# First attention pass of a four-layer graph network: where the second half of a batch is packed and turned

## The chip, the cores and the metric

The kernel runs on one core of one Trainium2 chip. The metric is the device time of one execution in microseconds; three executions of the kernel before gave 8632.77, 8639.03 and 8645.94 us, median 8639.03 us.

## The reference, cut to what matters

Four graph layers run one after another over 6250 nodes of 128 features and 106250 edges, each followed by a residual and a layer norm. The second one, a graph attention with 4 heads of 64 features, is the one the change touches:

```python
h = (x @ W).reshape(n, HEADS, HID)                      # 4 heads x 64
e = jax.nn.leaky_relu(a_src[src] + a_dst[dst], 0.2)
m = jax.ops.segment_max(e, dst, num_segments=n)
ex = jnp.exp(e - m[dst])
denom = jax.ops.segment_sum(ex, dst, num_segments=n)
msg = h[src] * (ex / denom[dst])[:, :, None]
agg = jax.ops.segment_sum(msg, dst, num_segments=n)
```

## The kernel before, in words

Edges were sorted earlier into chunks of 128 by their target's tile of 128 nodes. `attend_running` (line 1222) goes over all chunks once, in 58 batches (`NB`) of 8 pairs of chunks (`BP`), 16 chunks a batch (`BC`). It keeps a running maximum per target, so that for each batch two kinds of work are in flight: the maxima and scores of batch b, and the messages and sums of batch b-1. Five instruction streams are written out by hand, one for each engine, and are tied together by semaphores; each engine runs its stream strictly in the order written.

**GpSimd** gathers the source rows of a batch by 16 indirect DMAs (L1350), into a ring of three batches; each half of 8 waits until the sums of the batch three before have left the ring. **SyncE** loads hot bytes (L1323) and bit lines (L1331).

**For the maxima of batch b**: ScalarE copies the source part of a half batch out of the gathered rows (`pack(b, n)`, L1514, n = 0 or 1 for the half), TensorE transposes it in two matmuls (`turn(b, n)`, L1600), ScalarE copies the result to SBUF (`line(b, n)`, L1523). Then, for each pair a of 0 to 7, TensorE spreads the lines over all lanes in 8 matmuls (`spread(b, a)`, L1614; pairs 0 to 3 need `line(b, 0)`, pairs 4 to 7 `line(b, 1)`), VectorE reduces the 128x1024 result (`reduce`, L1390) and takes it into the running maximum (`top`, L1398). PSUM holds two pairs, so a spread waits for the reduce two before. After the last pair VectorE makes the shifts (`shift`, L1404 to L1412, and `change`, L1421), TensorE expands them to the edges in 48 small matmuls (`expand`, L1625), VectorE makes the scores (L1443 to L1449) and ScalarE the exponentials (L1544, L1545). ScalarE also widens the hot bytes (`widen` L1531, `hot` L1536).

**For the sums of batch b-1**: ScalarE multiplies three heads of each chunk by their weights (`message(b - 1, a)`, L1553, 6 instructions for a pair, 48 for a batch), VectorE the fourth (L1454); TensorE sums a pair in 4 float matmuls (`total(b - 1, a)`, L1640), VectorE adds the sum to the accumulator (`add`, L1462). A total waits for its messages and for the add two before.

The order in one turn of the loop before the change:

- ScalarE: messages 0 and 1, `pack(b, 1)`, message 2, `line(b, 1)`, messages 3 to 7, `pack(b + 1, 0)`, `hot(b)`, `line(b + 1, 0)`, `widen(b + 1)`, a small exponential, then the exponentials of batch b.
- TensorE: for a = 2 to 7 `spread(b, a)` and `total(b - 1, a - 2)`, with `turn(b, 1)` ahead of spread 4; then totals 6 and 7, `turn(b + 1, 0)`, spreads 0 and 1 of b + 1, `expand(b)`.
- VectorE: for a = 2 to 7 reduce a, top a-1, add a-2; top 7, the shifts, adds 6 and 7, reduces 0 and 1 of b + 1, the scores, its part of the messages, `rescale` (L1431, L1434).

Of the kernel before, what the change touches and what calls it, by code (L numbers as in the profile page):

```python
# [83 lines left out]
def gnn_resnorm_kernel(nc, x_in, src_in, dst_in, type_in, rfeat, relw, loopw,  # L84
# [3 lines left out]
    with ctx:  # L88
# [1133 lines left out]
        def attend_running(name, f, t_tab, a_src, a_dst, most):  # L1222
# [6 lines left out]
            BP = 8  # L1229
            BC = 2 * BP  # L1230
            HALF = BC // 2
            NB = NPAIR // BP
# [5 lines left out]
            with Phase() as ph:  # L1238
# [51 lines left out]
                def rows_gathered(b):  # L1290
                    return (b // ZR + 1) * 16 * HALF

                def loaded_pairs(b, slots):
                    return (b // slots + 1) * 16 * BP

                def turned(b, n):
                    at = n * P
                    return ps[0:PR, 6 + b % 2, at:at + P].bitcast(bf16)
# [17 lines left out]
                with nc.Block() as block:  # L1316
                    @block.sync
                    def _(sp):
                        def bytes_in(b):
                            if b >= HR:  # L1320
                                sp.wait_ge(s_hot, b - HR + 1)
                            for a in range(BP):
                                sp.dma_start(hb[:, b % HR, a], hb_tab[:, bass.ds(places[b][a], 2), :])\  # L1323
                                  .then_inc(s_hb[b % HR], 16)

                        def bits_in(b):
                            if b >= 2:
                                sp.wait_ge(s_spread, (b - 1) * BP)
                            for a in range(BP):
                                at = PR + a % 2 * 2 * LB  # L1330
                                sp.dma_start(lines[at:at + 2 * LB, b % 2, a // 2, :],  # L1331
                                             bit_tab[bass.ds(places[b][a], 2)].rearrange("c k e -> (c k) e"))\
                                  .then_inc(s_bits[b % 2], 16)

                        places = {}
                        for b in range(-2, NB):
                            if b + 2 < NB:
                                places[b + 2] = registers([mybir.EngineType.SP], pair_at, b + 2, NCH - 2)
                                bytes_in(b + 2)
                            if 0 <= b + 1 < NB:  # L1340
                                bits_in(b + 1)
                                places.pop(b + 1)
# [159 lines left out]
                    @block.scalar  # L1502
                    def _(act):
                        for n in range(2):
                            act.wait_ge(s_pt, n + 1)
                            nc.scalar.activation(pick[:, n * HALF:(n + 1) * HALF, :].rearrange("p m e -> p (m e)"),
                                                 ps[0:LR, 4 + n, :].bitcast(bf16), ACT.Copy).then_inc(s_pick, 1)

                        def pack(b, n):
                            at = 2 * b + n  # L1510
                            act.wait_ge(s_gath[b % ZR][n], rows_gathered(b))
                            if at >= 2:
                                act.wait_ge(s_turn, at - 1)
                            nc.scalar.activation(  # L1514
                                parts[:, n, :].rearrange("p (c w) -> p c w", w=HP),
                                ring[:, b % ZR].bitcast(bf16)[:, n * HALF:(n + 1) * HALF, 2 * W:2 * RW], ACT.Copy)\
                              .then_inc(s_pack, 1)

                        def line(b, n):
                            act.wait_ge(s_turn, 2 * b + n + 1)  # L1520
                            if b >= 2:
                                act.wait_ge(s_spread, (b - 1) * BP)
                            nc.scalar.activation(  # L1523
                                lines[0:PR, b % 2, n * QB // 2:(n + 1) * QB // 2, :].rearrange("p q e -> p (q e)"),
                                turned(b, n), ACT.Copy).then_inc(s_line, 1)

                        def widen(b):
                            act.wait_ge(s_hb[b % HR], loaded_pairs(b, HR))
                            if b >= WR:
                                act.wait_ge(s_exp, b - WR + 1)  # L1530
                            nc.scalar.activation(wide[:, b % WR], hot_bytes(b, 0), ACT.Copy).then_inc(s_wide, 1)  # L1531

                        def hot(b):
                            if b >= WR:
                                act.wait_ge(s_sum, (b - WR + 1) * BP)
                            nc.scalar.activation(hots[:, b % WR], hot_bytes(b, P), ACT.Copy).then_inc(s_hot, 1)  # L1536

                        def fading(b):
                            act.wait_ge(s_diff, b)
                            nc.scalar.activation(fade[:, b % 2, :], fade[:, b % 2, :], ACT.Exp).then_inc(s_fade, 1)  # L1540

                        def exponential(b):
                            act.wait_ge(s_sc, 3 * b + 3)
                            nc.scalar.activation(factors(b), score[:, b % 2], ACT.Exp).then_inc(s_e, 1)  # L1544
                            nc.scalar.activation(ring[:, b % ZR, :, hf:W], score[:, b % 2], ACT.Exp).then_inc(s_e, 1)  # L1545

                        def message(b, a):
                            if a == 0:
                                act.wait_ge(s_e, 2 * b + 2)
                            for c in range(2 * a, 2 * a + 2):  # L1550
                                for h in range(ACT_HEADS):
                                    r = ring[:, b % ZR, c, h * f:(h + 1) * f]
                                    last = nc.scalar.activation(r, r, ACT.Copy,  # L1553
                                                                scale=ring[:, b % ZR, c, hf + h:hf + h + 1])
                            last.then_inc(s_ma, 1)

                        pack(0, 0)
                        line(0, 0)
                        widen(0)
                        for b in range(NB + 1):  # L1560
                            for a in range(BP):
                                if b < NB and a == 2:
                                    pack(b, 1)
                                if b < NB and a == 3:
                                    line(b, 1)
                                if b >= 1:
                                    message(b - 1, a)
                            if b + 1 < NB:
                                pack(b + 1, 0)
                            if b < NB:  # L1570
                                hot(b)
                            if b + 1 < NB:
                                line(b + 1, 0)
                                widen(b + 1)
                            if 1 <= b < NB:
                                fading(b)
                            if b < NB:
                                exponential(b)
                            if b == NB - 1:
                                act.wait_ge(s_of, 1)  # L1580
                                nc.scalar.activation(own[:], own[:], ACT.Exp).then_inc(s_og, 1)

                    @block.tensor
                    def _(pe):
# [64 lines left out]
                        for b in range(NB + 1):  # L1649
                            for a in range(2, BP):  # L1650
                                if b < NB:
                                    if a == BP // 2:
                                        turn(b, 1)
                                    spread(b, a)
                                if b >= 1:
                                    total(b - 1, a - 2)
                            if b >= 1:
                                total(b - 1, BP - 2)
                                total(b - 1, BP - 1)
                            if b + 1 < NB:  # L1660
                                turn(b + 1, 0)
                                spread(b + 1, 0)
                                spread(b + 1, 1)
                            if b < NB:
                                expand(b)
                            tiles.pop(b, None)
                            if b + 1 < NB:
                                tiles[b + 1] = registers(PE_ENGINE, pair_tile, b + 1, NT)
# [973 lines left out]
```

## Time and profile before

| | before |
|---|---|
| median of three executions | 8639.03 us |
| the profiled execution, its own time | 8636.3 us |
| its span in the trace | 8634.5 us |
| first exponential of the pass to the last | 2496.02 to 3747.14 us |
| busy share over the whole span: TensorE, VectorE, ScalarE, GpSimd | 62%, 66%, 35%, 71% |

The shares are means over a dozen stages with different limits; the pass in question takes about 15% of the span. A time in the trace counts from the start of the span. A row of a stretch gives its ends and its length, then the busy time of TensorE's matmuls, its weight loads, VectorE, ScalarE and GpSimd with their instructions in brackets, the granted clock of TensorE as a share of full speed, the share of busy DMA engines and GB/s. What stands in brackets at the end of a row of the timeline is the idle time of the engine just before it, and what ended it.

### The profile page before, as it was taken

The page shows a single profiled execution, that of the slowest core. Times are in us where ns is not written, and L with a number is a line of the kernel's source. Part 1 is how long each engine was busy: PE and PEld are TensorE (multiplying, and loading weights), DVE is VectorE, ACT ScalarE, POOL GpSimd, SP SyncE. Part 2 cuts the span into 40 slices and gives each one's busy share as a digit, 9 for nine tenths or more (in the row PEclk, how much of TensorE's full clock was granted, in tenths as well). Part 3 has the DMA queues.
Part 4 walks back from the last instruction along what each step waited for, and adds up shares of the span by engine and source line. Part 5 has one row for each costly group of instructions (what it writes and reads, how often), then busy time and mean ns, then how long its engine had stood idle before and what let it go on. Part 6 is the DMA issues. An engine that isn't in the chain of part 4 may idle for free. (4 is left out here: it accounts for less than half of the span.)

```text
span 8634.5 us, 137054 instructions
## 1 busy us (share of the span) xinstructions
PE 5332.5 (62%) x37070; PEld 4681.0 (54%) x37070; DVE 5717.4 (66%) x14044; ACT 2990.4 (35%) x6453; POOL 6115.6 (71%) x5619
## 2 busy tenths in 40 slices
PE   0991014444368888854444425666569898989896
PEld 0340013333356666643333315565569898989896
DVE  9660025555577777774444455555579898989898
ACT  2000002000047777742222222222246565655564
POOL 4777767777547767726777727777768787878785
PEclk6995555555577777776666657667889999999998
DMA  1771025565644444533333334444467676767674
GB/s 42 274 308 45 2 52 130 131 145 131 109 120 132 130 128 130 122 59 89 81 80 82 82 44 129 129 129 129 126 163 221 190 222 189 221 188 219 189 222 138
DMA packets 963001, 1176.45 MB, mean 136 GB/s; under 512 B 286475, under 2 KB 845279, under 8 KB 949199
## 3 DMA queue, kind: packets, MB, share of 16 engines
q1 hardware_dynamic: 806638, 864.50, 32.7%
q0 software_dynamic: 155616, 303.19, 16.3%
q8 instruction: 324, 5.31, 0.3%
q14 instruction: 423, 3.46, 0.1%
HBM read 897.16 MB, written 269.96 MB: 135 GB/s over the span
## 5 line engine op out<-in xcount | busy, mean ns | idle before, releaser
L2560 PE MATMUL ps<-u,wide_r 128*128 x9280 | 1140.1, 277 | 129.5 <-issue 88.7
L2391 POOL TENSOR_TENSOR msg_r<-zo_r,share_r 128x1024 f32<-128x1024 f32 x580 | 1122.0, 1934 | 101.6 <-DVE share_r L2450 45.8
L2560 PEld LDWEIGHTS ps<-u,wide_r 128*128 128x128 f32 x9280 | 1091.8, 193 | 131.4 <-issue 131.4
L2572 PE MATMUL ps<-msg_r,hots_r 128*128 128x128 f32 x9280 | 1140.6, 276 | 24.5 <-POOL msg_r L2391 23.3
L1350 POOL DMA_INDIRECT ring_e<-t_tab,src_p x928 | 878.2, 946 | 386.2 <-issue 267.2
L2133 POOL DMA_INDIRECT z_r<-x_tab,src_row x880 | 856.0, 973 | 417.0 <-issue 267.9
L2572 PEld LDWEIGHTS ps<-msg_r,hots_r 128*128 128x128 f32 x9280 | 1081.8, 192 | 33.5 <-POOL msg_r L2391 32.5
L295 POOL DMA_INDIRECT rec_tab<-pay,row_i x831 | 805.6, 969 | 375.1 <-issue 274.6
L583 POOL DMA_INDIRECT ring<-y_tab,y_row x880 | 839.5, 954 | 306.4 <-issue 264.5
L1753 POOL DMA_INDIRECT ring_e<-t_tab,src_row x880 | 830.4, 944 | 271.9 <-issue 271.9
L2399 POOL TENSOR_TENSOR prod_r<-prod_r 128x512 f32<-128x512 f32 x580 | 734.4, 1266 | 320.5 <-DVE prod_r L2422 307.0
L842 PE MATMUL ps<-ring,hots 128*128 128x129 f32 x1760 | 453.2, 438 | 697.5 <-issue 533.3
L842 PEld LDWEIGHTS ps<-ring,hots 128*128 128x128 f32 x1760 | 394.3, 329 | 756.5 <-issue 618.1
L2275 PE MATMUL ps<-unit,wide_r 128*128 x1760 | 399.1, 419 | 583.2 <-ACT wide_r L2240 578.8
L2461 DVE TENSOR_TENSOR u_sum<-ps,u_sum 128x128 f32 x2320 | 671.8, 290 | 103.1 <-PE ps L2572 22.2
L2422 DVE TENSOR_TENSOR prod_r<-ps,zo_r 128x1024 f32<-128x1024 f32 x580 | 705.4, 1216 | 34.4 <-PE ps L2560 30.9
L2275 PEld LDWEIGHTS ps<-unit,wide_r 128*128 128x128 f32 x1760 | 368.9, 319 | 603.5 <-issue 603.5
L1640 PE MATMUL ps<-ring_e,hots_e 128*128 128x260 f32 x1856 | 627.3, 471 | 94.4 <-ACT ring_e L1553 89.5
L1553 ACT ACTIVATE ring_e<-ring_e 128x64 f32<-128x64 f32 x2784 | 681.4, 334 | 1.9
L2512 ACT ACTIVATE wide_r<-zo_r 128x1024 f32<-128x1024 uint8 x580 | 605.4, 1044 | 97.8 <-PE ps L2560 62.0
L1390 DVE TENSOR_REDUCE high_e<-ps 128x4 f32<-128x1024 f32 x464 | 560.7, 1219 | 100.1 <-PE ps L1614 98.8
L2524 ACT ACTIVATE hots_r<-zo_r 128x1024 f32<-128x1024 uint8 x580 | 603.5, 1040 | 0.0
(317 smaller groups left out, 9472.1 us busy)
## 6 DMA issues: line engine op xcount, KB each, us to landing
zo_r<-zo_tab SPq DMA_DIRECT2D x2320, 192.0 KB, 2.8
y_tab<-wide SPq DMA_DIRECT2D x100, 1024.0 KB, 3.9
zo_tab<-z_r SPq DMA_DIRECT2D x110, 512.0 KB
hot_bytes_e<-hb_tab SPq DMA_DIRECT2D x464, 64.0 KB
dl_b<-dl_tab SPq DMA_DIRECT2D x220, 128.0 KB, 3.7
zo_tab<-hot_bytes SPq DMA_DIRECT2D x220, 128.0 KB
hb_tab<-hot_bytes SPq DMA_DIRECT2D x220, 128.0 KB
hot_bytes_e<-hb_tab SPq DMA_DIRECT2D x55, 512.0 KB
```

What stands on the lines that cost most here:

```text
L295: nc.gpsimd.indirect_dma_start(out=rec_tab, out_offset=bass.IndirectOffsetOnAxis(ap=row_i[:, j:j + 1], axis=0), in_=pay[:, j, :], in_offse ...
L583: nc.gpsimd.indirect_dma_start(out=ring[:, s, c, 0:width], out_offset=None, in_=table, in_offset=bass.IndirectOffsetOnAxis(ap=rows[:, q * ...
L842: last = nc.tensor.matmul(sum_of(s, c), hots[:, s, c, :], ring[:, s, c, :], start=True, stop=True)
L1350: nc.gpsimd.indirect_dma_start(out=ring[:, b % ZR, c, :], out_offset=None, in_=t_tab, in_offset=bass.IndirectOffsetOnAxis(ap=src_p[:, b * ...
L1753: nc.gpsimd.indirect_dma_start(out=ring[:, b % ZR, c, :], out_offset=None, in_=t_tab, in_offset=bass.IndirectOffsetOnAxis(ap=src_row[:, b ...
L2133: nc.gpsimd.indirect_dma_start(out=z[:, g % ZR, c, :], out_offset=None, in_=x3_tab, in_offset=bass.IndirectOffsetOnAxis(ap=src_row[:, g * ...
L2275: last = nc.tensor.matmul(ps[:, 2 * (g % 2) + c // 4, c % 4 * D:(c % 4 + 1) * D], wide[:, g % WR, c, :], unit[:, bass.ds(tiles[at // CQ, a ...
L2391: nc.gpsimd.tensor_tensor(msg[:, g % WR].rearrange("p c (k d) -> p c k d", d=CD), z_of(g).rearrange("p c (k d) -> p c k d", d=CD), share[: ...
L2399: nc.gpsimd.tensor_tensor(prod[:, :, 0:CD // 2], prod[:, :, 0:CD // 2], prod[:, :, CD // 2:CD], ALU.add).then_inc(s_half, 1)
L2422: v.tensor_tensor(prod[:].rearrange("p (c k) d -> p c (k d)", k=CAPS), up, z_of(g), ALU.mult).then_inc(s_prod, 1)
L2560: last = nc.tensor.matmul(ps[:, 2 * (g % 2) + c // 4, c % 4 * D:(c % 4 + 1) * D], wide[:, g % WR, c, :], u[:, bass.ds(tiles[g % NO % 4 * O ...
L2572: last = nc.tensor.matmul(ps[:, 4 + g % 2, c // 2 * D:(c // 2 + 1) * D], hots[:, g % WR, c, :], msg[:, g % WR, c, :], start=c % 2 == 0, st ...
```

## The change

On ScalarE `pack(b, 1)` and `line(b, 1)` move from between the messages to the head of the turn, ahead of message 0. On TensorE `turn(b, 1)` moves from ahead of spread 4 to ahead of spread 2. No instruction is added, removed or altered; the waits within each function stay as they are.

```diff
@@ ScalarE
                         for b in range(NB + 1):
-                            for a in range(BP):
-                                if b < NB and a == 2:
-                                    pack(b, 1)
-                                if b < NB and a == 3:
-                                    line(b, 1)
-                                if b >= 1:
+                            if b < NB:
+                                pack(b, 1)
+                                line(b, 1)
+                            if b >= 1:
+                                for a in range(BP):
                                     message(b - 1, a)
@@ TensorE
                         for b in range(NB + 1):
                             for a in range(2, BP):
                                 if b < NB:
-                                    if a == BP // 2:
+                                    if a == 2:
                                         turn(b, 1)
                                     spread(b, a)
```

## Rows read from the trace of the kernel before

**Rows 1.** Waits of ScalarE in the pass: total us, times, longest.
```profile
ACT lines_e L1523 <- PE ps L1600: 125.6, 78, 2.9
...
ACT slot_parts_e L1514 <- DMA ring_e<-t_tab,src_p: 18.8, 3, 6.9
```

**Rows 2.** Groups, pass: count | busy us, mean ns | idle, releasers.
```profile
L1350 POOL DMA_INDIRECT ring_e<-t_tab,src_p x928 | 878.2, 946 | 386.2 <-issue 267.2 <-PE ps L1640 102.9 <-POOLq L109 16.1
```

**Rows 3.** Timeline of ScalarE, 52 batches apart: start, duration.
```profile
2518.79 0.23 ACT L1544 ACTIVATE ps<-score_e 128x64 f32<-128x64 f32 x1 [2.80 <-DVE score_e L1449]
...
3642.58 0.23 ACT L1544 ACTIVATE ps<-score_e 128x64 f32<-128x64 f32 x1 [2.73 <-DVE score_e L1449]
```

**Rows 4.** Timeline of ScalarE in batch A, from one exponential to the next.
```profile
2949.89 0.23 ACT L1544 ACTIVATE ps<-score_e 128x64 f32<-128x64 f32 x1 [2.77 <-DVE score_e L1449]
...
2950.32 2.97 ACT L1553 ACTIVATE ring_e<-ring_e 128x64 f32<-128x64 f32 x12
...
2957.08 0.38 ACT L1523 ACTIVATE lines_e<-ps 48x256 bf16<-48x256 bf16 x1 [2.19 <-PE ps L1600]
2957.36 7.25 ACT L1553 ACTIVATE ring_e<-ring_e 128x64 f32<-128x64 f32 x30
...
2967.64 0.38 ACT L1523 ACTIVATE lines_e<-ps 48x256 bf16<-48x256 bf16 x1 [1.05 <-PE ps L1600]
...
2972.72 0.23 ACT L1544 ACTIVATE ps<-score_e 128x64 f32<-128x64 f32 x1 [2.81 <-DVE score_e L1449]
```

**Rows 5.** Timeline, start of the pass: one pack, its turn, its line.
```profile
2469.15 0.28 ACT L1514 ACTIVATE slot_parts_e<-ring_e 128x96 bf16<-128x96 bf16 x1 [5.67 <-DMA ring_e<-t_tab,src_p]
2469.48 0.41 PE L1600 MATMUL ps<-ident_b,slot_parts_e 128*48 128x128 bf16 x2 [7.12 <-ACT slot_parts_e L1514]
2469.93 0.38 ACT L1523 ACTIVATE lines_e<-ps 48x256 bf16<-48x256 bf16 x1 [0.50 <-PE ps L1600]
```

**Rows 6.** Timeline of TensorE in batch A.
```profile
2951.91 2.10 PE L1640 MATMUL ps<-ring_e,hots_e 128*128 128x260 f32 x4 [1.32 <-ACT ring_e L1553]
2953.81 1.06 PE L1614 MATMUL ps<-lines_e,pick_e 104*128 104x128 bf16 x8
2954.66 2.05 PE L1640 MATMUL ps<-ring_e,hots_e 128*128 128x260 f32 x4
...
2957.52 1.03 PE L1614 MATMUL ps<-lines_e,pick_e 104*128 104x128 bf16 x8 [0.47 <-ACT lines_e L1523]
2958.34 2.04 PE L1640 MATMUL ps<-ring_e,hots_e 128*128 128x260 f32 x4
2960.18 1.06 PE L1614 MATMUL ps<-lines_e,pick_e 104*128 104x128 bf16 x8
```

**Rows 7.** Timeline of TensorE in batch B, after A.
```profile
2979.91 0.62 PE L1614 MATMUL ps<-lines_e,pick_e 104*128 104x128 bf16 x8 [0.47 <-ACT lines_e L1523]
2980.37 1.09 PE L1640 MATMUL ps<-ring_e,hots_e 128*128 128x260 f32 x4
2981.30 0.61 PE L1614 MATMUL ps<-lines_e,pick_e 104*128 104x128 bf16 x8
```

**Rows 8.** Timeline of VectorE: reduce 7 (A), reduces 4 and 7 (B).
```profile
2964.49 1.22 DVE L1390 TENSOR_REDUCE high_e<-ps 128x4 f32<-128x1024 f32 x1
...
2980.57 1.23 DVE L1390 TENSOR_REDUCE high_e<-ps 128x4 f32<-128x1024 f32 x1 [0.77 <-PE ps L1614]
...
2985.20 1.21 DVE L1390 TENSOR_REDUCE high_e<-ps 128x4 f32<-128x1024 f32 x1
```

**Rows 9.** Stretches of A, A, B, C; 1.00 or 0.50 is the granted clock.
```profile
2951.91:2961.60 9.69, 9.22 (x40) 6.87 (x41) 5.31 (x10) 7.50 (x32) 5.35 (x6) 0.50 0.40 103
2961.80:2971.80 10.00, 9.35 (x101) 7.41 (x100) 9.05 (x20) 7.06 (x17) 6.94 (x8) 1.00 0.44 121
2974.75:2978.70 3.95, 3.95 (x15) 3.19 (x16) 2.45 (x4) 2.98 (x13) 3.02 (x4) 0.50 0.47 119
2995.87:2999.20 3.33, 3.33 (x14) 2.67 (x15) 1.83 (x4) 2.98 (x13) 2.58 (x3) 0.50 0.53 135
```

## The prediction

> **What bounds the kernel now.** I read the waits of ScalarE in the pass first: the engine that the change reorders loses 125.6 us to waits of a line for its turn, in 78 of the 116 lines (two in each of 58 batches) [rows 1]. Then its timeline, to see which line waits where. In batch A `line(b, 1)` stops ScalarE for 2.19 us in the middle of the messages, because TensorE's `turn(b, 1)` stands behind totals 0 and 1; at the end of the turn `line(b + 1, 0)` stops it for 1.05 us more and the exponential for 2.81 us [rows 4]. So ScalarE is not the only bound: in A it ends its messages and stands waiting for TensorE and VectorE. Last come TensorE's timeline and its clock. The first totals run at a granted 0.50 of full speed (1.2 GHz) and the later ones at 1.00 (2.4 GHz) [rows 9]. The period of a batch is the length of one loop over these three engines. From the exponential at 2518.79 to that at 3642.58 there are 52 batches, so 1123.79 / 52 = 21.61 us each [rows 3]; A has 22.83 [rows 4]. GpSimd takes (878.2 + 267.2) / 928 = 1.234 us for a gather and its issue gap, near 20 us for 16 with the gaps that the waits hide, and it waits 102.9 us for totals to free the ring [rows 2]. It follows the loop and sets a floor of about 20.0 us a batch.
>
> **The change part by part.** All times below count from the exponential of the batch.
>
> *ScalarE's head.* Before, message 0 starts at 2950.32 - 2949.89 = 0.43 [rows 4]. Now pack and line stand there. The price of the pair with nothing in TensorE's way is shown once, at the start of the pass: pack to line is 2469.93 - 2469.15 = 0.78, with the turn (0.41, at the low clock) inside [rows 5]; line to the next instruction is 2957.36 - 2957.08 = 0.28 [rows 4]. Message 0 starts at 0.43 + 0.78 + 0.28 = 1.49, which is 1.06 later. The pack should find its gathered rows there: of 116 packs three waited for a gather, all in the filling of the pass [rows 1, 5]. TensorE is free for the turn, having nothing to do between the expand and total 0 but spread 2.
> All 48 messages and the gap behind them then run without a stop. In A the last 30 messages, the next pack and `hot` end 2967.64 - 1.05 - 2957.36 = 9.23 after they begin [rows 4]; 18 more messages at 7.25 / 30 = 0.242 are 4.35. ScalarE could start `line(b + 1, 0)` at 1.49 + 4.35 + 9.23 = 15.07. Before, in A, it was free at 16.70 and served at 17.75. ScalarE alone gains 1.6 us in such a batch.
>
> The Trainium skill ("Advanced Engine Details and Errata", Network/Comms) says that a sequencer takes 50 to 100 ns to read a semaphore. The two hand-overs in the rows of the pass's start show 0.05 and 0.04 us; by the page's upper figure the head would be 0.1 us longer, and an estimate from it takes some 5 us off the gain.
>
> *TensorE's chain.* Before, total 0 starts 2951.91 - 2950.32 = 1.59 after message 0 [rows 4, 6]; now at 1.49 + 1.59 = 3.08, against 2.02. From there at the low clock: total to spread 2953.81 - 2951.91 = 1.90, spread to total 0.85, so spread 3 at 4.98 and total 1 at 5.83. Before, spread 4 waited for turn and line and came 2957.52 - 2954.66 = 2.86 after total 1, in A at 7.63. Now spread 4 follows total 1 at once, at the low clock after 2960.18 - 2958.34 = 1.84 and at the high clock after 2981.30 - 2980.37 = 0.93 [rows 6, 7]. At the low clock all along it would be at 7.67, no earlier than before. So the gain hangs on when the clock rises. That is the crux: the change starts the totals 1.06 later and removes the 0.47 idle of TensorE behind the turn [rows 6].
>
> *When the clock rises.* Three batches repeat over and over. In B the granted clock stays 0.50 from total 0 at 2974.75 for 3.95, in C from 2995.87 for 3.33, and is 1.00 behind it, as in the second stretch of A; in A it lasts 9.7, from 2951.91 to 2961.6 [rows 9]. In the low part of B and C TensorE is busy throughout (3.95 of 3.95, 3.33 of 3.33), in A 9.22 of 9.69. A's idle is the 0.47 behind the turn, that in B and C came just after the rise. With the turn at the head, TensorE has no idle after total 0 while it is slow, since messages come every 1.45 and a slow pair takes 1.90 + 0.85. I take C's value, 3.4, and B's 4.0 as the other end; A's 9.7 is the bad bound. A middle value, and mixes, are among the rivals.
> With 3.4 the clock rises at 6.48. Total 1, begun at 5.83, has done 0.65 of 1.84, 35%; the rest takes 0.65 x 0.93 = 0.60; spread 4 at 7.08.
>
> *VectorE's chain.* Reduce 4 comes 2980.57 - 2979.91 = 0.66 after spread 4 [rows 7, 8], at 7.74. Reduce 7 comes 2985.20 - 2980.57 = 4.63 later at the high clock, at VectorE's own pace of reduce, top and add. From reduce 7 of A to the next exponential it is 2972.72 - 2964.49 = 8.23 [rows 4, 8]: the last adds, totals and turn, line, two spreads, the expand and the scores, with nobody ahead waiting for ScalarE's messages. The period is 7.74 + 4.63 + 8.23 = 20.6; batches whose expand runs some 0.1 faster make it 20.5, and I take 20.5. By ScalarE: line at 15.07, and from line to exponential 2972.72 - 2967.64 = 5.08, 20.15; by GpSimd 20.0. So what ends last is VectorE's chain behind the clock's rise, and ScalarE and GpSimd are close under it. With B's 4.0 the same steps give spread 4 at 7.38 and 20.8.
>
> *The sum.* (21.61 - 20.5) x 52 = 57.7 us. At the start of the pass gathers come one by one, and the first `pack(1, 1)` at the head holds message 0 until its rows are there: before, it came 0.43 + 2.9 (12 messages) after its exponential without waiting, so at most 3 us of delay, of which 2 are given back by the stop that goes; I take 1 us off. The last four batches are ruled by loads that come late, and I give them nothing. Net 57 us. What hides the moved work elsewhere: SyncE's loads are issued behind `hot` and the last spreads and have most of a batch before they are used; I cost them at nothing, and at up to 0.5 us a batch should bit lines come late for spread 0.
> The profiled execution is 8636.3 us (span 8634.5 and 1.8 around it); less 57 it is 8579.3. The median of the three runs shown is 2.7 above it, so I forecast 8582.
>
> **The rivals.**
> *The clock keeps its present points from the exponential, 5.4, 6.0 and 11.8, in turn.* They are the slow stretches of C, B and A behind a total 0 that began at 2.02 [rows 9]. For it: the three of them repeat through the pass. Against it: the idle of A is gone. At 5.4 total 1 begins at 5.6, spread 4 at 6.6, reduce 4 at 7.2: 20.1; at 6.0: 20.4; at 11.8 spread 5 is at 7.67 + 0.85 + 1.84 = 10.36, total 3 at 11.21 and spread 6 at 12.5, reduce 6 at 13.15, reduce 7 at 14.7: 22.9. Mean 21.1, gain 0.5 x 52 = 26, 8613.
> *Nothing to be seen.* The same, with one batch in three still 9.7 us from total 0 to the rise: then reduce 7 is at 15.2 and the batch 23.4; with 20.5 and 20.8 the mean is 21.6, gain 0, 8639. A floor by another engine would also end here; what speaks against the moved line being off the path everywhere is that 38 of the 116 lines do not wait at all [rows 1]; in those batches ScalarE's messages end last.
> *Slower: the later start keeps the clock low.* Total 0 begins 1.06 later after each exponential, and the clock, which falls around the expand, gets no earlier start. If the rise comes 6.8 after total 0 in every batch (halfway between C's and A's), at 9.9: total 2 begins at 8.5, has done 76% by then, spread 5 at 10.1, reduce 5 at 10.8, reduce 7 at 13.9, period 22.1. That is 0.5 x 52 = 26 us slower, 8665. It decides from a mean rise of about 5.7 after total 0 on. For it: A shows that a rise may be late. Against it: A is the one batch in three with an idle in it.
> *GpSimd's floor*: if the clock were never low, 20.0, gain 83, 8556.
> *The edit does not do what it says*: excluded as far as order goes, each engine runs what is written; but if line 1 waited at the head for more than 0.78, every 0.1 costs 5 us.
>
> **How the numbers follow.** Forecast 0.44, its own range 8570 to 8600 (20.3 to 20.8); clock at its old points 0.27; GpSimd's floor 0.02; nothing to be seen 0.12; slower 0.15. The range for 8 in 10 leaves out the slower case and the floor's far side and reaches over most of the "nothing" case: 8562 to 8640. What a measurement of this kernel can tell from no change is about 0.2%, 17 us. Faster by more: 0.44 + 0.27 + 0.02 = 0.73; same 0.12; slower 0.15.
>
> **What would show it.** Right: `line(b, 1)` 0.78 behind its pack; total 0 about 3.1 after the exponential; no idle of TensorE between total 0 and total 5; a granted clock of 1.00 from 3.4 to 4 us behind total 0 in all batches; exponentials 20.5 apart; ScalarE waiting a little at `line(b + 1, 0)` in every batch; GpSimd's wait for totals near 0.5 a batch. Wrong: low clock for 6 us or more behind total 0 in many batches, reduce 4 later than 8.5, or a pack that waits for a gather in the steady loop.

## The result, and the profile after

The changed kernel takes 8587.72 us (median, 8580.39 to 8594.27) against 8641.34 (8632.77 to 8645.94) for the kernel before in the same series: ratio 0.9940, 95% interval 0.9925 to 0.9954. The forecast was 8582. The profiled execution took 8590.03 us (span 8588.2), 46.3 less than the profiled one of before.

ScalarE in one batch of the changed kernel, from exponential to exponential (answers to [rows 4]):

```profile
2989.70 0.23 ACT L1544 ACTIVATE ps<-score_e 128x64 f32<-128x64 f32 x1 [2.82 <-DVE score_e L1449]
...
2990.01 0.27 ACT L1514 ACTIVATE slot_parts_e<-ring_e 128x96 bf16<-128x96 bf16 x1
2990.77 0.38 ACT L1523 ACTIVATE lines_e<-ps 48x256 bf16<-48x256 bf16 x1 [0.50 <-PE ps L1599]
2991.05 11.55 ACT L1553 ACTIVATE ring_e<-ring_e 128x64 f32<-128x64 f32 x48
...
3005.09 0.38 ACT L1523 ACTIVATE lines_e<-ps 48x256 bf16<-48x256 bf16 x1 [0.52 <-PE ps L1599]
...
3010.16 0.23 ACT L1544 ACTIVATE ps<-score_e 128x64 f32<-128x64 f32 x1 [2.80 <-DVE score_e L1449]
```

The second pack and line stand at the head, 0.76 apart, and the 48 messages are one row without a stop. TensorE in the same batch (answers to [rows 6, 7]):

```profile
2990.32 0.41 PE L1599 MATMUL ps<-ident_b,slot_parts_e 128*48 128x128 bf16 x2 [1.50 <-ACT slot_parts_e L1514]
2990.67 1.03 PE L1613 MATMUL ps<-lines_e,pick_e 104*128 104x128 bf16 x8
2992.63 2.10 PE L1639 MATMUL ps<-ring_e,hots_e 128*128 128x260 f32 x4 [0.93 <-ACT ring_e L1553]
2994.53 1.06 PE L1613 MATMUL ps<-lines_e,pick_e 104*128 104x128 bf16 x8
2995.38 1.46 PE L1639 MATMUL ps<-ring_e,hots_e 128*128 128x260 f32 x4
2996.68 0.61 PE L1613 MATMUL ps<-lines_e,pick_e 104*128 104x128 bf16 x8
```

Total 0 at 2992.63 and spread 3 run at the low clock, total 1 is faster in its second half (1.46, between 2.05 and 1.09), spread 4 at 2996.68 is fast. The two reduces of VectorE that the forecast went through, 4 and 7 (answers to [rows 8]):

```profile
2997.34 1.22 DVE L1390 TENSOR_REDUCE high_e<-ps 128x4 f32<-128x1024 f32 x1
...
3001.96 1.21 DVE L1390 TENSOR_REDUCE high_e<-ps 128x4 f32<-128x1024 f32 x1
```

Stretches of the same batch: length, then busy us of PE, PEld, DVE, ACT, POOL, the granted clock, DMA share, GB/s (answers to [rows 9]):

```profile
2992.78:2996.00 3.22, 3.22 (x14) 2.55 (x15) 1.05 (x4) 3.22 (x15) 2.31 (x4) 0.50 0.39 100
2996.30:3009.00 12.70, 11.80 (x121) 9.35 (x119) 11.67 (x25) 10.54 (x32) 9.15 (x11) 1.00 0.47 129
```

Before, the low stretch behind total 0 lasted 3.3, 3.95 and 9.7 us, in turn [rows 9]. Now all 53 batches of the steady loop show the short one: the granted clock rises 3.1 to 3.7 us behind total 0, 3.5 in the mean, where the mean of before was 5.7. The distances tell the same: before, the rises came 20.48, 27.31 and 17.07 us apart, in turn (their mean is the 21.6 of the batches); now all 52 distances are 20.48. A rise is here the point from which the trace has the granted clock at 1.00 in place of 0.50.

Waits of ScalarE in the pass (total us, times, longest; answers to [rows 1]), and the group of the gathers (answers to [rows 2], one row fewer in the window):

```profile
ACT ps L1544 <- DVE score_e L1449: 194.3, 57, 33.2
ACT lines_e L1523 <- PE ps L1599: 60.5, 113, 1.5
...
ACT slot_parts_e L1514 <- DMA ring_e<-t_tab,src_p: 24.3, 5, 8.5
```
```profile
L1350 POOL DMA_INDIRECT ring_e<-t_tab,src_p x927 | 877.9, 947 | 305.1 <-issue 270.0 <-PE ps L1639 35.1
```

ScalarE's waits for a turn fell from 125.6 to 60.5 us and are now 0.5 each in nearly every line. GpSimd's waits for totals fell from 102.9 to 35.1. But the exponential now has one wait of 33.2 us, which no batch of before had (the longest there was 14.1). The exponentials, 52 batches apart and then at the end of the pass (answers to [rows 3]):

```profile
2518.42 0.23 ACT L1544 ACTIVATE ps<-score_e 128x64 f32<-128x64 f32 x1 [2.80 <-DVE score_e L1449]
...
3583.48 0.23 ACT L1544 ACTIVATE ps<-score_e 128x64 f32<-128x64 f32 x1 [2.70 <-DVE score_e L1449]
...
3660.86 0.23 ACT L1544 ACTIVATE ps<-score_e 128x64 f32<-128x64 f32 x1 [33.24 <-DVE score_e L1449]
...
3702.15 0.23 ACT L1544 ACTIVATE ps<-score_e 128x64 f32<-128x64 f32 x1 [4.07 <-DVE score_e L1449]
```

The steady loop: (3583.48 - 2518.42) / 52 = 20.48 us a batch, against 21.61. That is 1123.79 - 1065.06 = 58.7 us gained. The last four batches: 3702.15 - 3583.48 = 118.67, against 3747.14 - 3642.58 = 104.56. That is 14.1 us given back. What else differs, 0.4 before the loop and 1.3 behind the pass, makes up the 46.3.

What the end of the pass waits for, in the changed kernel: SyncE's loads of the bit lines of the last two batches (8 for each), TensorE's first two spreads of the last batch but one, and the first of GpSimd's last 16 gathers.

```profile
3614.93 33.63 SPq L1331 DMA_DIRECT2D lines_e<-bit_tab  x16
```
```profile
3656.07 1.87 PE L1613 MATMUL ps<-lines_e,pick_e 104*128 104x128 bf16 x16 [30.77 <-issue]
```
```profile
3620.12 0.94 POOL L1350 DMA_INDIRECT ring_e<-t_tab,src_p  x1 [6.68 <-PE ps L1639]
```

And the same places of the kernel before, with the first two spreads of the batch ahead of it too:

```profile
3676.46 27.59 SPq L1331 DMA_DIRECT2D lines_e<-bit_tab  x16
```
```profile
3669.80 1.87 PE L1614 MATMUL ps<-lines_e,pick_e 104*128 104x128 bf16 x16 [11.93 <-issue]
...
3699.66 1.86 PE L1614 MATMUL ps<-lines_e,pick_e 104*128 104x128 bf16 x16 [8.83 <-issue]
```
```profile
3685.52 0.94 POOL L1350 DMA_INDIRECT ring_e<-t_tab,src_p  x1 [13.26 <-PE ps L1640]
```

Stretches of the changed kernel's end (columns as above):

```profile
3600.00:3610.00 10.00, 4.25 (x67) 3.86 (x68) 4.49 (x9) 1.79 (x5) 7.56 (x9) 0.51 0.99 87
3630.00:3640.00 10.00, 0.00 (x0) 0.00 (x0) 0.00 (x0) 0.00 (x0) 7.57 (x8) 0.50 1.02 96
3640.00:3650.00 10.00, 0.00 (x0) 0.00 (x0) 0.00 (x0) 0.00 (x0) 0.00 (x0) 0.50 0.99 85
```

The DMA engines are fully busy and move only 85 to 96 GB/s, where in the loop they move 129 at a share of 0.47. The last three batches of the pass (48 gathers) hold no edges; all their lanes are blanks, and every blank gathers one and the same row, 6272. TensorE computes nothing from 3630 to 3650: its next instruction is a spread that needs bit lines, and these are loaded while the DMA engines are full. Before, GpSimd waited 13.26 us for a total when it came to its last 16 gathers, and issued the first of them 9.1 us after the first load of these bit lines, when 5 of the 8 for the waiting batch were issued; the spread came 23.2 us after that first load. Now its wait is 6.68, the first of the 16 comes 5.2 us after the first load, when 3 of the 8 are issued, and the spread comes after 41.1 us. That the gathers hold the bit lines up, and more so the earlier they come, is a reading of the rows; the blanks' experiments below test that it needs the repeated row, and none tests the order of the two queues by itself.

### The profile page after: what moved, and what is told of

The parts are those of the page before. It is cut to its first block and busy times, and to the rows that moved or that the text cites. A ratio compares the mean times of both kernels' runs of the same rounds, so it can differ in the third digit from the quotient of the medians.

```text
span 8588.2 us, 137054 instructions
## 1 busy us (share of the span) xinstructions
PE 5273.9 (61%) x37070; PEld 4651.3 (54%) x37070; DVE 5706.2 (66%) x14044; ACT 2989.6 (35%) x6453; POOL 6115.9 (71%) x5619
## 3 DMA queue, kind: packets, MB, share of 16 engines
q0 software_dynamic: 155616, 303.19, 16.6%
## 5 line engine op out<-in xcount | busy, mean ns | idle before, releaser
L2571 PE MATMUL ps<-msg_r,hots_r 128*128 128x128 f32 x9280 | 1140.5, 276 | 24.4 <-POOL msg_r L2390 23.2
L1639 PE MATMUL ps<-ring_e,hots_e 128*128 128x260 f32 x1856 | 582.6, 447 | 81.0 <-ACT ring_e L1553 55.7
```

What stands on the lines that cost most here:

```text
L2571: last = nc.tensor.matmul(ps[:, 4 + g % 2, c // 2 * D:(c // 2 + 1) * D], hots[:, g % WR, c, :], msg[:, g % WR, c, :], start=c % 2 == 0, st ...
```

## Experiments

"Loop" is the mean distance of exponentials over the 52 batches, "end" the last four, both from the profiled execution. The changed kernel has 20.48 and 118.67, the kernel before 21.61 and 104.56. Each time is a median with its ratio to the kernel before on the same chip; that kernel measured 8637.13 (10 runs) beside the turn alone, the later line, the first filling of the head and the filling of A's idle; 8640.89 (11) beside the blanks on the kernel before; 8641.73 (9) beside the others.

**The turn alone.** From the kernel before; ScalarE's order stays old.

```diff
-                                    if a == BP // 2:
+                                    if a == 2:
                                         turn(b, 1)
```

> TensorE's half of the change alone: turn(b, 1) ahead of spread 2, ScalarE's order as before, with pack(b, 1) behind message 1 and line(b, 1) behind message 2. Theory (the gain is a chain: ScalarE's head, total 0, spread 4 and the clock's rise): the turn stands first in TensorE's queue and waits for the pack at 3.3 behind the exponential, so spread 2 and total 0 come at about 4.1 and 5.1 in place of 2.0, spread 4 near 9; batches near 22.7 us, the kernel some 50 us slower than before. Rival (what counts is only that the turn stands early, so that line(b, 1) does not wait): the waits of line(b, 1) fall from 1.8 to under 0.2 us and the kernel is 40 to 60 us faster, as the full change.

8675.3 us, ratio 1.0041 (1.0026 to 1.0057); loop 22.26, end 121.13. TensorE at the head of a batch:

```profile
3009.89 0.41 PE L1600 MATMUL ps<-ident_b,slot_parts_e 128*48 128x128 bf16 x2 [4.44 <-ACT slot_parts_e L1514]
3010.23 1.03 PE L1614 MATMUL ps<-lines_e,pick_e 104*128 104x128 bf16 x8
3011.06 2.05 PE L1640 MATMUL ps<-ring_e,hots_e 128*128 128x260 f32 x4
```

The exponential was at 3006.26. The turn waits for the pack, which comes behind 12 messages, and total 0 starts 4.80 behind the exponential, where it was 2.02. So half of the change costs 38 us; it pays only with ScalarE's half. The size was forecast too large: loop batches alternate near 22.6 and 21.7. The clock rose mostly near 4.2 and 2.1 us behind total 0, in turn, not 3.4 in each. ScalarE's half cannot run alone: `line(b, 1)` ahead of message 0 would wait for a turn that stands behind totals 0 and 1, and these wait for messages 0 and 1.

**The line one message later.** From the changed kernel: the pack stays at the head, the line goes behind message 0, so that message 0 doesn't wait.

```diff
-                                line(b, 1)
-                            if b >= 1:
-                                for a in range(BP):
+                            for a in range(BP):
+                                if b < NB and a == 1:
+                                    line(b, 1)
+                                if b >= 1:
                                     message(b - 1, a)
```

> The changed kernel with line(b, 1) behind message 0 on ScalarE; pack(b, 1) and the turn stay at the head. The 0.5 us wait at the head goes, message 0 starts at 0.61 behind the exponential and total 0 at 2.2 in place of 3.1. Theory A (a plain chain behind the exponential): the clock rises 3.4 behind total 0, spread 4 comes 0.9 us earlier, the batch is 19.6 by VectorE and so held at GpSimd's 20.0: 0.4 to 0.5 us a batch or 20 to 25 us less than the changed kernel. Theory B (the loop falls in step with the clock: in the changed kernel 52 batches took 20.48 each and the rises come at the same distance, whatever the chain allows): exponentials stay 20.48 apart, the clock rises later behind total 0 (about 4.3) and the time is that of the changed kernel within 5 us.

8574.39 us, ratio 0.9924 (0.9910 to 0.9937); loop 20.30, end 121.87. Between the two expectations. Total 0 comes 2.06 behind the exponential (2.93 in the changed kernel), so 0.87 was freed at the head, and the loop got 0.18 of it. The clock tells why. Two stretches from total 0 to the rise, of neighbouring batches (columns as above):

```profile
3311.88:3317.10 5.22, 5.22 (x22) 4.08 (x23) 3.27 (x6) 5.22 (x23) 4.00 (x5) 0.50 0.46 108
...
3332.23:3334.20 1.97, 1.97 (x5) 1.40 (x6) 1.28 (x2) 1.97 (x9) 1.36 (x3) 0.50 0.40 121
```

In most batches the clock rises 4.9 to 5.3 us behind total 0, where theory A had 3.4 and theory B 4.3: total 0 comes 0.87 earlier and the rise some 0.9 later after the exponential. These batches take 20.2 to 20.7. Of the 52 distances of rises 49 are still 20.48, and three are 17.07. With each of the three a burst comes: here 20.35, then 19.12 (the second stretch), 19.54, 19.88, 20.16, and 20.45 again, while the rise comes 2.0, 3.3, 4.3 and 4.9 behind total 0. So theory B had the direction right, with the bursts as an exception. 19.12 is below the 20.0 that the prediction gave as GpSimd's floor, so that is no floor of a single batch.

**More work for TensorE at the head.** From the changed kernel: 14 spare matmuls into unused columns behind the expand and 8 ahead of total 0, so that TensorE idles less before the totals.

```diff
+                                if b + 1 < NB:
+                                    fill(14, 6 + (b + 1) % 2, 448)
...
+                                    if a == 2 and 2 <= b < NB:
+                                        pe.wait_ge(s_acc, adds_done(b - 2, 6))
+                                        fill(8, 4, 384)
```

> The changed kernel with idle TensorE time filled by matmuls whose results nobody reads: 14 of 64 columns behind the expand and 8 of 128 columns ahead of total 0. If the low clock behind total 0 is what holds the batch (VectorE's chain behind the clock's rise), the clock rises near or before total 0, spread 4 comes near 6.0 in place of 7.0 and the batch falls to ScalarE's 20.15 or GpSimd's 20.0: 15 to 25 us less than the changed kernel. If TensorE's clock is not what holds the batch, the fillers only stand in the way: no gain, or up to 0.5 us a batch slower (25 us).

8583.35 us, ratio 0.9938 (0.9924 to 0.9951); loop 20.44, end 115.5. Total 0 and total 1 of a batch in mid-pass:

```profile
3003.77 0.57 PE L1605 MATMUL ps<-ident_b 128*128 128x64 bf16 x14
3005.35 0.41 PE L1599 MATMUL ps<-ident_b,slot_parts_e 128*48 128x128 bf16 x2 [1.01 <-ACT slot_parts_e L1514]
...
3006.51 1.06 PE L1605 MATMUL ps<-ident_b 128*128 128x128 bf16 x8
3007.66 2.10 PE L1644 MATMUL ps<-ring_e,hots_e 128*128 128x260 f32 x4
3009.55 1.06 PE L1618 MATMUL ps<-lines_e,pick_e 104*128 104x128 bf16 x8
3010.40 1.45 PE L1644 MATMUL ps<-ring_e,hots_e 128*128 128x260 f32 x4
```

The same 2.10 and 1.45 as without the spare matmuls: the clock rises at the same place. 1.01 of idle was left ahead of the turn, so the run did not test a head without idle. The first batches were short, 19.96, 19.85, 20.02, 20.32 and 20.19, and from the sixth on they took 20.3 to 20.7. In the first the clock rose 1.1 us behind total 0:

```profile
2518.51:2519.55 1.04, 1.04 (x3) 0.85 (x4) 0.46 (x2) 1.04 (x6) 0.78 (x1) 0.50 0.44 102
```

In the next four it rose 1.8, 2.5, 2.9 and 3.1 us behind total 0, then 3.2 to 3.7. All 52 distances of rises are 20.48, those of the short batches too: each short batch brings total 0 that much earlier before the next rise. A heavier filling came next.

> The changed kernel with 24 and 9 fillers in place of 14 and 8; in the weaker one TensorE still idled 1.0 us ahead of the turn, the clock fell and rose as without fillers, and batches went from 19.9 at the start to 20.48 within ten batches. Theory of the step (batches shorter than 20.48 move the loop against the clock until the low stretch costs as much as they gained): the same again, a start with batches under 20.2 and then 20.48, unless the clock no longer falls at all, and then 20.0 to 20.2 throughout. Rival (plain chain): every batch 20.0 to 20.2, some 18 us less than the changed kernel.

With 24 and 9 in place of 14 and 8: 8584.64 us, ratio 0.9935 (0.9919 to 0.9950); loop 20.48, end 118.2. The 24 took 0.90, and 0.68 of idle stayed. No gain. In two of the first twelve batches the clock rose before total 0, and these took 19.72; the loop as a whole gained nothing.

**The idle of A filled, in the old order.** From the kernel before: four spare matmuls behind `turn(b, 1)`, where TensorE idled 0.47.

```diff
                                         turn(b, 1)
+                                        if b >= 1:
+                                            pe.wait_ge(s_acc, adds_done(b - 1, 0))
+                                            fill(4, 4, 384)
```

> The kernel before, its order unchanged, with 4 matmuls of 128 columns that nobody reads behind turn(b, 1), in the 0.47 us in which TensorE waited for line(b, 1). Theory (that idle kept the clock low in one batch of three, and this is part of what the change gains): the batches of 22.83 go, all take 20.9 to 21.1, mean 20.95, some 34 us less than before. Rival (the idle does not matter, the long batches come from the place of the loop relative to the clock): the three-batch pattern stays, mean 21.6, time as before within 10 us.

8608.39 us, ratio 0.9968 (0.9955 to 0.9982); loop 21.33, end 104.0.

```profile
3008.83 0.29 PE L1600 MATMUL ps<-ident_b,slot_parts_e 128*48 128x128 bf16 x2
3009.06 0.40 PE L1606 MATMUL ps<-ident_b 128*128 128x128 bf16 x4
3009.60 0.62 PE L1619 MATMUL ps<-lines_e,pick_e 104*128 104x128 bf16 x8
```

The idle is gone (0.14 left), and with it the batches of 22.83: the exponentials now come 21.6, 21.65, 21.2 and 20.8 apart. The clock now rises 6.4, 5.3, 4.1 and 3.4 behind total 0, in turn, where the longest was 9.8. The loop gains (21.61 - 21.33) x 52 = 14.6 us, a quarter of the change's 58.7. By the medians the run gains 28.7, not far from the 34 expected; of what the profiled execution gains (23.0) 5.3 lie ahead of the pass, which the edit does not touch, so this part of the kernel varies by that much. The other 44 of the loop come from the order. An estimate splits the 58.7 by the batches of before in which the rise came as early as after the change: C's took 20.87 with the rise at 3.3, the changed kernel's 20.48 with it at 3.5. Had all batches of before been like C, the loop had gained (21.61 - 20.87) x 52 = 38 us; the shorter path at the same rise is the other 20.

**The blanks spread over rows.** From the changed kernel: a blank of lane p gathers row 6272 + p (as many rows, all alike) in place of row 6272. In short (two instructions of VectorE outside the pass in place of one):

```diff
+ src_g = (src_f == 0) * part
- src_p = src_f + float(NT * P)
+ src_p = (src_f + float(NT * P)) + src_g
```

> The changed kernel with the blank slots of this pass gathering 128 different rows (row 6272 + lane, all alike) in place of row 6272 for every lane. Between the exponentials 53 and 57 the changed kernel takes 118.7 us and the kernel before 104.6, where four batches at 20.48 would be 82: the part of the expected gain that did not come. Theory (the gathers of the last three batches, all blanks, read one row over and over, which holds the DMA engines, and the bit lines of the last batches wait behind them, longer in the changed kernel because GpSimd issued the last batch's gathers ahead of them): DMA share in the tail falls from 0.97 to about 0.6, the tail takes 82 to 85 us, 30 to 35 us less than the changed kernel. Rival (it is the bytes, or SyncE's queue): the tail stays within 5 us.

8554.59 us, ratio 0.9899 (0.9884 to 0.9914); loop 20.54, end 81.44, so 37.2 less at the end. Stretches of the end:

```profile
3600.00:3610.00 10.00, 7.64 (x80) 6.14 (x78) 7.11 (x15) 6.82 (x26) 7.58 (x8) 0.69 0.61 165
3610.00:3620.00 10.00, 9.11 (x64) 6.89 (x64) 9.39 (x21) 9.38 (x33) 7.39 (x8) 0.97 0.41 109
3620.00:3630.00 10.00, 7.59 (x85) 5.99 (x84) 7.07 (x14) 6.70 (x24) 7.56 (x9) 0.71 0.40 112
```

The gathers are as many and as large; the DMA share falls from 1.0 to 0.4 to 0.6, and the last four batches take 20.0 to 20.6 each.

The start of this pass shows something else, for here the clock rose late in the first batches. From total 0 to the rise, in the first batch and in the seventh:

```profile
2518.94:2525.10 6.16, 6.16 (x26) 4.92 (x27) 3.02 (x7) 6.16 (x27) 4.64 (x6) 0.50 0.42 115
...
2644.45:2648.00 3.55, 3.55 (x14) 2.88 (x15) 1.39 (x4) 3.55 (x16) 2.64 (x4) 0.50 0.44 120
```

With the rise at 6.2, 5.1, 4.4, 3.9, 3.7, 3.6 and 3.6 behind total 0 the batches took 22.23, 21.18, 20.93, 20.66, 20.59, 20.52 and 20.50, and all rises came 20.48 apart. So the length of a batch follows the clock's rise, as in the prediction's chain, and the loop moves until its batches are as long as the rises are apart: here from above, in the run with the head filled from below.

**The same edit on the kernel before.**

> The kernel before with the blank slots of this pass spread over 128 rows. It takes the tail out of the comparison of the two orders: the changed kernel with the same edit takes 81.4 us from exponential 53 to 57 and 8554.6 us in all. If the tail's loss is what parts the measured gain from the forecast one: the batches stay at 21.61, the tail falls from 104.6 to 86 to 88, the kernel to about 8620, and the change is worth 62 to 66 us between these two, against 54 between the two without the edit. Rival (the tail's difference was chance of one execution): about 8605 and a difference near 54 as before.

8613.01 us, ratio 0.9968 (0.9955 to 0.9980); loop 21.64, end 85.05. With both ends freed, the change is worth 8613.01 - 8554.59 = 58.4 us (medians of two series, on the same chip), where with the blanks on one row it is 53.6. The expectation had 62 to 66 and its rival 54, and the intervals of the two ratios (11 to 13 us each way) cannot part 58.4 from either: the medians leave it open. The profiled executions do say more. The end costs the change 14.1 us with the blanks on one row and gives it 3.6 with them spread; and with the blanks on one row the five runs with the turn at the head have ends of 115.5 to 121.9, the two with the old order 104.6 and 104.0, so that this is no chance of one execution.

**Together.** The line behind message 0 and the spread blanks:

> Line(b, 1) behind message 0 and the spread blanks together. If the two are independent: the mean batch of 20.3 of the one and the tail of the other, 10 + 33 us less than the changed kernel, near 8545. If the tail is another for a loop that reaches it at another point: more or less than that by up to 10.

8536.96 us, ratio 0.9881 (0.9866 to 0.9896); loop 20.13, end 78.27. That is 8 us less than the sum of the two. The loop is shorter than the 20.30 of the later line alone: six distances of rises are 17.07 here, three there.

And the blanks of the other gather passes too; the blank records, which named one row for all lanes, now name one for each. In short, without the semaphores:

```diff
-v.memset(pay[:, 0:NCH // 2, 1:2], NT * P)
+nc.gpsimd.iota(pay[:, 0:NCH // 2, 0], pattern=[[0, NCH // 2]], base=0, channel_multiplier=1)
+nc.gpsimd.iota(pay[:, 0:NCH // 2, 1], pattern=[[0, NCH // 2]], base=NT * P, channel_multiplier=1)
```

> As the kernel with line(b, 1) behind message 0 and spread blanks, but all blank records point to different rows, so that the blank gathers of the three other passes that gather rows spread too. In each of them the DMA share stands at 0.9 to 1.0 in the last 20 to 30 us of gathers against 0.25 to 0.6 earlier. Theory of the repeated row: each tail gets 5 to 20 us shorter, 20 to 40 us in all beyond the kernel with this pass alone, near 8515. Rival (those tails are bound by GpSimd's issue): nothing beyond it.

8496.66 us, ratio 0.9834 (0.9820 to 0.9847), the fastest here: 40.3 below the last, the upper end of what was expected. In the profiled executions 23.9 us of it lie ahead of the pass (first exponential at 2470.28 against 2494.16) and 16.6 behind it; the pass itself is 3.8 longer. One stretch at the end of another gather pass, first in the changed kernel:

```profile
2310.00:2320.00 10.00, 3.39 (x14) 3.15 (x15) 2.76 (x7) 0.00 (x0) 7.56 (x9) 0.50 0.97 64
```
and with all blanks spread:
```profile
2310.00:2320.00 10.00, 4.31 (x17) 3.58 (x16) 5.63 (x14) 0.00 (x0) 7.59 (x8) 0.50 0.48 128
```

Twice the GB/s at half the share.

## Why the prediction was right, and where it was not

- *The head.* Forecast: pack to line 0.78, message 0 at 1.49, total 0 at 3.08. Measured from 2989.70: 0.76, 1.35, 2.93. The pack starts at 0.31, not 0.43: it follows the exponential's second half sooner than a message does. The hand-overs took 0.04 us each way. The Trainium skill ("Advanced Engine Details and Errata", Network/Comms) has 50 to 100 ns for a sequencer's read of a semaphore; the trace does not show such a read by itself, but whole hand-overs that are shorter (the end of a matmul is modelled).
- *TensorE and the clock.* Forecast: spread 3 at 4.98, total 1 at 5.83, the rise 3.4 behind total 0, spread 4 at 7.08. Measured 4.83, 5.68 and 6.98. Total 1's 1.46 lies between the 2.05 and 1.09 of the two levels, which puts the rise 0.79 after its start (0.79 + (2.05 - 0.79) x 1.09 / 2.05 = 1.46), 3.5 behind total 0. This was the crux, and its number held in all 53 batches (3.1 to 3.7). That a late rise is what lengthens a batch is borne out too, by the starts of the runs with the spread blanks and with the head filled. But that the value was 3.4 was in part luck. I took it from C as a time from total 0 to the rise, as if total 0 set it off. It is mostly 4.9 to 5.3 where total 0 comes 0.87 earlier, 4.2 and 2.1 in turn where it comes at 4.80, and 1.1 to 6.2 at the starts of passes in the same order. It is 3.5 because there a batch is 20.48 us long, the distance of the rises. That the idle behind the turn is what made batch A long is shown in part: filling it alone removed the 22.83 batches, though not the whole difference.
- *VectorE.* Forecast: reduce 4 at 7.74, reduce 7 at 12.37, the next exponential at 20.5. Measured 7.64, 12.26, and 20.46 in this batch, 20.48 over the loop. The chain of steps came to 20.6, and I rounded it down; that it met the distance of the rises, 20.48, so closely is luck as well, for a head 0.87 shorter took only 0.18 off.
- *GpSimd.* Forecast 0.5 of waiting a batch; measured 35.1 / 58 = 0.6.
- *The loop.* Forecast 57.7 us, measured 58.7.
- *The start of the pass.* I took 1 us off for a pack that waits for its gathers at the head. The first distance of exponentials grew from 22.77 to 23.45, and the waits of packs for gathers from 3 to 5 (18.8 to 24.3 us).
- *The last four batches.* "I give them nothing" was the mis-sized term: they lost 14.1 us. I had called their loads late and left it there. The row that should have stopped me was in the trace of before, in its last batches:

```profile
3680.00:3690.00 10.00, 9.22 (x60) 6.60 (x59) 8.39 (x18) 8.12 (x33) 3.56 (x4) 0.90 0.95 103
```

A DMA share of 0.95 at 103 GB/s, where A's first stretch moved the same 103 at 0.40 [rows 9]. With the DMA engines that full, the order in which GpSimd and SyncE issue could not be costed at nothing.

By the profiled executions the forecast of 57 was 10.7 too high: 14.1 for the end, less 1.0 for the loop, 1.4 for the start and 1.3 behind the pass, and 0.3 of rounding. By the medians it was 3 too high.

Of the rivals, the clock at its old points (8613), no change (8639) and slower (8665) lie outside the measured interval. The slower one asked for a mean rise 5.7 us or more behind total 0; it was 3.5. That rival has a slip: halfway between C's 3.33 and A's 9.7 is 6.5, not 6.8, which makes it some 8 us less slow and changes nothing else. The turn alone ended slower too, but not by that rival's way: total 0 came late (4.80), while the clock rose 3.2 behind it in the mean.

What stays open: why the rises come 20.48 us apart, and now and then 17.07. The loop keeps to 20.48 because they do, and shortening the head further is mostly not paid out; which work of TensorE the clock answers to, no run shows.

## What to carry to other kernels

- A stop that two engines share goes only if it is moved on both: the turn alone cost 38 us, both together gained 54.
- Work out the ends of a pass apart from its loop, from the DMA share and the GB/s there: where the share is near 1.0 at few GB/s, a change of the order in which engines issue is not free; here it moved the end by 14.1 us.
- Look at the clock's rises in several batches, and at the start of a pass, before a time from one event to the rise is taken as fixed.
- Give padding lanes rows of their own. Blanks that all gather one row cost this kernel some 73 us (33.1 in this pass, 40.3 in the others), more than the change brought.

## What the runs showed of the hardware

- Gathers in which all lanes read one row kept the 16 DMA engines at a share of 0.91 to 1.02 while they moved 39 to 96 GB/s; spread over 128 rows, the same gathers took 0.40 to 0.61 at 109 to 165 GB/s.
- The granted clock and the loop went in step: in all 53 batches of the changed kernel it rose 3.1 to 3.7 us behind total 0, and all 52 distances of rises were 20.48. They were so from the first batch on in runs whose first batches took 22.23 or 19.96: the loop came to the clock. A head that was 0.87 shorter gave batches of 19.1 to 20.3 only for four at a time, behind a distance of 17.07, and otherwise 20.2 to 20.7.
- Small matmuls that fill idle time (0.57 and 0.90 us of them a batch behind the expand) did not move the point at which the clock rose in the steady loop, only in a few of the first twelve batches. Four of them (0.40 us) in the idle of the old order brought the latest rise from 9.8 to 6.4 us behind total 0.
